# A two-layer sandwich of masked and sign-binarised projections: mask blocks spread on VectorE, and another order of the first unit

## What is computed

```python
# x: (2, 8192, 4096) f32; w1, w2: 4096 x 4096 f32; mask: 4096 x 4096 int32, constant over 32 x 32 blocks
block_mask = mask.reshape(128, 32, 128, 32).sum(axis=(1, 3)) > 0
w1m = w1 * repeat(block_mask, 32 rows, 32 columns)
x = x + layernorm(layernorm(x) @ w1m.T)
x = x + layernorm(layernorm(x) @ sign(w2).T + bias)
```

## Time and profile before

| | us |
|---|---|
| median of 3 runs | 1957.43 (1955.93 to 2028.07) |
| the profiled execution, own time | 1950.22 |
| its span, slowest core | 1948.7 |
| TensorE busy with matmuls | 1859.5 (95%) |
| VectorE busy | 967.1 (50%) |
| ScalarE busy | 484.5 (25%) |
| GpSimd busy | 230.6 (12%) |

### The profile page before, as it was taken

The page is one execution under the profiler, slowest core; times in us unless marked ns, Lnnn a source line. Parts: engine busy times, 40 slices in busy tenths (PEclk is TensorE's granted clock), DMA queues, the critical chain, the costliest instruction groups (busy, mean ns, idle before and its releaser), DMA issues.

```text
span 1948.7 us, 26135 instructions; the slowest of 8 cores (1937.1 to 1948.7 us)
## 1 busy us (share of the span) xinstructions
PE 1859.5 (95%) x9483; PEld 875.6 (45%) x9483; DVE 967.1 (50%) x1441; ACT 484.5 (25%) x449; POOL 230.6 (12%) x420
## 2 busy tenths in 40 slices
PE   2689999999999999999999999999999999999996
PEld 1245444444444444444445444444444444444442
DVE  5778477666564330665533534433552333342465
ACT  2266300000000000133445444434420011110032
POOL 2444100000011000110101000000001011000110
PEclk8899999999999999999999999999999999999998
DMA  9998689976698764787799988898863566562494
GB/s 295 330 311 295 182 284 323 302 220 237 228 313 261 248 200 141 236 257 229 234 274 285 294 275 288 278 314 279 266 213 114 194 227 207 187 200 71 141 284 164
DMA packets 121791, 471.53 MB, mean 242 GB/s; under 512 B 13600, under 2 KB 13616, under 8 KB 106304
## 3 DMA queue, kind: packets, MB, share of 16 engines
q1 hardware_dynamic: 85248, 289.44, 47.4%
q0 software_dynamic: 36416, 180.41, 26.9%
HBM read 354.46 MB, written 115.34 MB: 241 GB/s over the span
## 4 chain that ended last, share of the span: by engine, by line
PE 83%; DMA 9%; DVE 3%; SPq 2%; issue 1%; POOL 1%; ACT 1%; DVEq 0%; ACTq 0%; POOLq 0%
PE pb L474 81%; DMA ST<-w2s 2%; DMA RING<-x 2%; DMA ST<-w1s 2%; PE pb L464 2%; DMA HT<-x 1%; DVE BNX L670 1%; SPq L383 1%; SPq L349 1%; DVE RING L662 1%; DVE RR L638 1%; DMA ST<-mask 0%; DMA ST<-x 0%; PE pb L456 0%; POOL HT L974 0%
## 5 line engine op out<-in xcount | busy, mean ns | idle before, releaser
L474 PE MATMUL pb<-RING,HT 128*128 128x512 bf16 (+1 forms) x8192 | 1786.8, 380 | 21.7 <-DVE RING L662 18.0
L474 PEld LDWEIGHTS pb<-RING,HT 128*128 128x128 bf16 x8192 | 800.3, 98 | 985.9 <-issue 37.8
L760 DVE TENSOR_TENSOR YS<-pb,RR 128x512 bf16<-128x512 f32 x112 | 77.3, 691 | 335.0 <-PE pb L474 334.9
L686 DVE BATCH_NORM_STATS2 BNST<-YS 128x6 f32<-128x512 bf16 x240 | 150.2, 682 | 152.7 <-ACT YS L847 151.5
L847 ACT ACTIVATE YS<-pb 128x512 bf16<-128x512 f32 x128 | 74.7, 600 | 539.7 <-PE pb L474 539.4
L662 DVE TENSOR_TENSOR RING<-ST,ME 128x1024 bf16<-128x1024 f32 x122 | 145.0, 1222 | 102.8 <-PE pb L474 70.4
L853 ACT ACTIVATE RING<-ST 128x1024 fp8e4<-128x1024 f32 x128 | 132.1, 1067 | 179.4 <-DMA ST<-w2s 179.2
L876 ACT ACTIVATE ST<-HT,NM,RS 128x2048 f32<-128x2048 bf16 x32 | 65.7, 2088 | 382.1 <-DVE NM L630 378.7
L638 DVE TENSOR_REDUCE RR<-ST 128x32 f32<-128x1024 int32 x120 | 142.4, 1212 | 25.1 <-DMA ST<-mask 24.3
L837 ACT ACTIVATE HT<-pb 128x1024 bf16<-128x1024 bf16 x128 | 122.3, 1041 | 130.6 <-PE pb L464 130.5
L743 DVE TENSOR_TENSOR HT<-HT,ST 128x1024 bf16<-128x1024 bf16 x64 | 75.6, 1223 | 90.6 <-DMA ST<-x 87.5
(11 more groups left out here) (53 smaller groups left out, 335.1 us busy)
## 6 DMA issues: line engine op xcount, KB each, us to landing
ST<-w2s SPq DMA_DIRECT2D x128, 512.0 KB, 12.5
ST<-w1s SPq DMA_DIRECT2D x122, 512.0 KB, 10.5
ST<-mask SPq DMA_DIRECT2D x120, 512.0 KB, 9.7
ST<-x POOLq DMA_DIRECT2D x64, 512.0 KB, 11.1
out<-ST POOLq DMA_DIRECT2D x32, 1024.0 KB, 6.9
HT<-x SPq DMA_DIRECT2D x24, 1024.0 KB, 20.6
y1d<-YS POOLq DMA_DIRECT2D x32, 512.0 KB, 4.4
c1d<-RING POOLq DMA_DIRECT2D x32, 512.0 KB, 9.0
```

The lines of the kernel that those rows point to most:

```text
L474: ins = t.matmul(bank(b), HT[:, c:c + 128], w[:, e * 512:(e + 1) * 512], start=(first and e == 0), stop=(last and e == 3))
L686: v.bn_stats(BNST[:, c:c + 6], YS[:, i * 512:(i + 1) * 512]).then_inc(sem["bns"], 1)
L760: v.tensor_tensor(YS[:, i * 512:(i + 1) * 512], bank(i), BIA[:, (slab % 2) * 512:(slab % 2) * 512 + 512], op=OP.add).then_inc(sem["ev2"], 1)
```

## The change

1. **Mask layout.** The host puts each 32x32 block of the mask on one partition (1024 numbers in a row), so one reduction gives one sum for a whole block: `mask_piece` writes a 128x1 column of MR. After every two pieces (after 16 for slabs 2 to 7) VectorE compares and repeats the sums over 32 columns (BW) and transposes BW in squares of 32x32 into ME. The matmuls with P4 and SEL, BT, BTD, RR and the semaphores between the engines are gone.
2. **START** no longer moves in units 2 to 7. It is 4 in units 2 to 16, where it was 4, 6, 0, 2, 4, 6 and then 0. In units 16 to 31 it is the old value plus four.
3. **Order of the start.** SyncE loads x tiles 0 to 7 first, then for each of the 8 blocks of slab 0 two mask and two weight pieces, then tiles 8 to 15, with four mask and four weight pieces (blocks 8 and 9) between them, and then the rest of slab 1 in the order mask, mask, weight, weight. TensorE transposes tiles 0 to 7, runs slab 0 over them block by block, and then runs tiles 8 to 15 one after another.
4. **Smaller things.** `x_stats` waits for each half of x by itself; `norm1` does not wait for `norm0`; the normalised halves of tiles 8 to 15 stay where the loaded half lay (`xnormed`); the transposes of tiles 0 to 7 alternate between banks 6 and 7; GpSimd spills unit 0 in one go after `norm1(8)`; `load_x(k, 1)` for tiles 14 and 15 waits until tile k-2 is transposed.

```diff
-
-MASK_END = {2: 2, 3: 3, 4: 4, 5: 5, 6: 6, 7: 7}
-
 START = {2: 4}
 for _u in range(2, 31):
-    if _u in MASK_END:
-        START[_u + 1] = (START[_u] + 2) % 8
-    elif 16 <= _u < 24:
+    if 16 <= _u < 24:
         START[_u + 1] = (START[_u] + 4) % 8
     else:
...
-STAGES = 13
+
+STAGES = 11
+EARLY = 6
...
+    for b in range(8):
+        for e, kind in enumerate("mmww"):
+            put((kind, 2 * b + e % 2), (4 * b + e) % 11)
...
-XHOME = [(k, 8 + k) for k in range(8)] + [(k, "TRW"[(k - 8) % 3]) for k in range(8, 16)]
-
-SEMS = (["cst", "msk_rd", "wgt", "sgn", "rdy_bt", "rdy_me", "msk_mm", "xaggr", "xstat", "xn0", "xn1",
+XHOME = ([(k, 8 + k) for k in range(8)] + [(k, 4 + k) for k in range(8, 12)]
+         + [(k, "TW"[k % 2]) for k in range(12, 16)])
...
-                if h == 0 and k >= 8:
-                    s.wait_ge(sem["xn1"], k - 7)
...
+                if k >= 8:
+
+                    o = k - 8 if k < 12 and h == 0 else k - 4 if k < 12 or h == 0 else k - 2
+                    if k >= 14 or h == 0 or k < 12:
+                        s.wait_ge(sem["tr"], 4 * o + 4)
+                    else:
+                        s.wait_ge(sem["msk_rd"], 16)
+                        s.wait_ge(sem["wgt"], 16)
...
-            load_x(0, 0)
-            load_x(0, 1)
-            for j in range(4):
-                for g in range(4 * j, 4 * j + 4):
-                    load_mask(g)
-                load_x(j + 1, 0)
...
+                            ).then_inc(sem[("ldX%d", "ldH%d")[h] % k], 16)
+
+            for k in range(8):
                 load_x(k, 0)
                 load_x(k, 1)
-            load_x(8, 0)
+            for b in range(8):
+                load_mask(2 * b)
+                load_mask(2 * b + 1)
+                load_w1(2 * b)
+                load_w1(2 * b + 1)
...
+                load_x(k, 0)
                 load_x(k, 1)
...
+                if k in (10, 12):
+                    load_mask(6 + k)
+                    load_mask(7 + k)
+                if k in (11, 13):
+                    load_w1(5 + k)
+                    load_w1(6 + k)
+            for kind, n in FEED[1][EARLY:]:
+                if kind == "m":
+                    load_mask(n)
...
-
-            def start_transposes(k, groups):
-                for g in groups:
-                    if g == 0:
-                        t.wait_ge(sem["xn0"], k + 1)
-                    if g == 2:
-                        t.wait_ge(sem["xn1"], k + 1)
-                    q = 4 * k + g
-                    if q >= 3:
-                        t.wait_ge(sem["tev"], q - 2)
-                    transposes(k, g, 4 + q % 3)
-
-            for j in range(4):
-                t.wait_ge(sem["msk_rd"], 4 * j + 4)
-                if j > 0:
-                    t.wait_ge(sem["rdy_me"], j)
-                mask_sums(7, 0, [j])
-                t.wait_ge(sem["rdy_bt"], j + 1)
-                t.matmul(pb[:, 7 * 512 + 128:7 * 512 + 256], SEL[:, :],
-                         BTD[:, j * 128:(j + 1) * 128], start=True, stop=True
-                         ).then_inc(sem["msk_mm"], 1)
...
+            def start_transposes(k, g):
+                if g == 0:
+                    t.wait_ge(sem["xn0"], k + 1)
+                if g == 2:
+                    t.wait_ge(sem["xn1"], k + 1)
+                q = 4 * k + g
+                if k < 8:
+                    if q >= 2:
+                        t.wait_ge(sem["tev"], q - 1)
+                elif k == 8:
+                    t.wait_ge(sem["ev1"], 4 + g + 1)
+                else:
+                    t.wait_ge(sem["tev"], q - 3)
+                transposes(xnormed(k, g // 2)[:, (g % 2) * 1024:(g % 2) * 1024 + 1024],
+                           6 + q % 2 if k < 8 else 4 + g)
+
+
+            for k in range(8):
+                for g in range(4):
+                    start_transposes(k, g)
+            for b in range(8):
+                for i in range(8):
+                    if b == 0:
+                        t.wait_ge(sem["tev"], 32 if i >= 6 else 4 * i + 4)
+                    if i == 0:
+                        wait_block_ready(t, b)
+                    ins = visit(i, i, b, b == 0, b == 7)
+                    if b == 7:
+                        ins.then_inc(sem["mm"], 1)
+
+            for g in range(4):
+                start_transposes(8, g)
+            for k in range(8, 16):
+                t.wait_ge(sem["ev1"], k - 7 if k < 12 else k - 3)
                 for b in range(8):
-                    if b == 1 and k < 15:
-                        start_transposes(k + 1, range(3))
-                    if b == 4 and k < 15:
-                        start_transposes(k + 1, (3,))
-                    if b == 3 and k == 15:
-                        t.wait_ge(sem["rdy_bt"], 5)
-                        t.matmul(bank(7), SEL[:, :], BTD[:, :], start=True, stop=True
-                                 ).then_inc(sem["msk_mm"], 1)
+                    if k < 15 and b in (3, 6):
+                        for g in ((0, 1) if b == 3 else (2, 3)):
+                            start_transposes(k + 1, g)
+                    if b % 2 == 0:
+                        t.wait_ge(sem["tev"], 4 * k + b // 2 + 1)
                     ins = visit(k % 4, k, b, b == 0, b == 7)
                     if b == 7:
                         ins.then_inc(sem["mm"], 1)
                     elif k == 15:
                         ins.then_inc(sem["blk"], 1)
-                if k == 14:
-                    t.wait_ge(sem["msk_rd"], 32)
-                    t.wait_ge(sem["rdy_me"], 4)
-                    mask_sums(7, 1, range(4))
...
-                        if b == 7 and p == 3 and u in MASK_END:
-                            s = MASK_END[u]
-                            t.wait_ge(sem["msk_rd"], 16 * s + 16)
-                            wait_acc_out(t, u, START[u])
-                            mask_sums(START[u], s, range(4))
-                if u in MASK_END:
-                    masks += 1
-                    t.wait_ge(sem["rdy_bt"], masks)
-                    wait_acc_out(t, u, (START[u] + 1) % 8)
-                    t.matmul(bank((START[u] + 1) % 8), SEL[:, :], BTD[:, :], start=True, stop=True
-                             ).then_inc(sem["msk_mm"], 1)
...
             def mask_piece(g):
-                s, q = g // 16, g % 16
+
+
+                at = g % 32
                 wait_stage_full(v, ("m", g))
-                if q == 0 and s >= 2:
-
-                    v.wait_ge(sem["msk_mm"], 7 if s == 2 else 9 + 2 * (s - 3))
-                v.tensor_reduce(RR[:, (s % 2) * 512 + q * 32:(s % 2) * 512 + q * 32 + 32],
-                                stage(("m", g), True).rearrange("p (a b) -> p a b", b=32),
-                                AX.X, OP.add).then_inc(sem["msk_rd"], 1)
-
-            def mask_bits(b, j0, nj):
-
-                edge(v.tensor_scalar(BT[:, j0 * 16:(j0 + nj) * 16],
-                                     pb[0:32, b * 512 + j0 * 16:b * 512 + (j0 + nj) * 16],
+                v.tensor_reduce(MR[:, at:at + 1], stage(("m", g), True), AX.X, OP.add
+                                ).then_inc(sem["msk_rd"], 1)
+                w = 2 if g < 32 else 16
+                if g % w < w - 1:
+                    return
...
+                v.wait_ge(sem["msk_rd"], g + 1)
+                edge(v.tensor_scalar(BW[:, 0:w * 32].rearrange("p (t i) -> p t i", i=32),
+                                     MR[:, at + 1 - w:at + 1].unsqueeze(2).broadcast_to([128, w, 32]),
                                      0.0, None, OP.is_gt))
-                dst = BTD[:, j0 * 128:(j0 + nj) * 128].rearrange("p (j k n) -> p j k n", j=nj, k=8)
-                bt = BT[:, j0 * 16:(j0 + nj) * 16].rearrange("p (j n) -> p j n", j=nj
-                                                             ).unsqueeze(2).broadcast_to([32, nj, 8, 16])
-                dk = DK[:, :].unsqueeze(1).unsqueeze(3).broadcast_to([32, nj, 8, 16])
-                v.tensor_tensor(dst, bt, dk, op=OP.mult).then_inc(sem["rdy_bt"], 1)
+                c = (g // 16 % 5) * 512 + (g % 16 + 1 - w) * 32
+                edge(v.transpose(ME[:, c:c + w * 32], BW[:, 0:w * 32]))
...
+            for k in range(8):
                 x_stats(k)
-                if k >= 8:
...
+            for b in range(8):
+                mask_piece(2 * b)
+                mask_piece(2 * b + 1)
+                weight_piece(2 * b)
+                weight_piece(2 * b + 1)
+            for k in range(8, 16):
+                x_stats(k)
+                y_stats(0, k - 8)
+                if k in (10, 12):
+                    feed1(FEED[1][3 * (k - 10) // 2:3 * (k - 10) // 2 + 2])
+                if k in (11, 13):
+                    feed1(FEED[1][3 * (k - 11) // 2 + 2:3 * (k - 11) // 2 + 3])
...
-            v.wait_ge(sem["xn1"], 16)
-            for kind, n in FEED[1]:
...
-            masks = 5
+            for b in range(2, 8):
+                feed1(FEED[1][3 * b:3 * b + 3])
+                if b < 6:
```

(31 more changed lines are left out.)

197 lines of the change are left out of this document (50 added, 147 removed).

## The result

The changed kernel takes 1937.74 us (median of 4 runs, 1937.42 to 1939.78). The ratio to before is 0.9905, 95% interval [0.9882, 0.9929], which is 18.6 us of 1957 (13.9 to 23.1). The forecast was 1933: 24.4 us off the median of 1957.4, of which 19.7 came. The profiled execution has a span of 1935.4 us on its slowest core (core 4), and its own time is 1937.42.

The account below looks back on a forecast made before the run. TensorE, busy 95% of the span, was taken to bound the kernel. Mask matmuls -10.2, an earlier unit 2 -15.9 and START +1.7 sum to -24.4 us, from the median of 1957.4 to 1933, range 1922 to 1944.

Parts of the forecast that it names:

- the wait itself: Unit 16, tile 7 now in fourth place instead of eighth: TensorE waits for its transposes' last eviction, +1.7 us.

Follow-up runs that it names:

- e10: Changed kernel with START 0 in units 4 to 16, e9's edits, 28 more identity matmuls a tile and four PSUM banks for early transposes; 1925.2 us, ratio 0.9855.
- e9: Changed kernel with e5's edits and GpSimd's spill(0) moved behind x_scale(9) and norm1(9); 1931.6 us, ratio 0.9883.
- e5: Changed kernel with unit 0's y_stats two tiles later and norm0(9) ahead of the last two evictions of tile 8's transposes; 1938.1 us, ratio 0.9892.

## What to carry to other kernels

A rotation or order table that is changed "by the way" has to be followed to every consumer of the order: here the place of one accumulator decided when a spill went out, and a chain behind it had no slack. A distance read on one core is only good if that core was on time there; read it on all of them. And a gain at the head is worth what the loads behind it let through: e10 started 6.4 us sooner than e9 and was done with unit 12, 740 us later, at the same time. So in this kernel the first change to make, after START, was the program order of GpSimd (one line on top of e5's edits, 3 to 5 us at unit 12 in the profiles), not the pace of the start.

## What the runs showed of the chip

- Around a wait of 2.63 or 2.64 us in unit 16 the clock fell on 7 of 8 cores (244 matmuls in 54.3 to 55.7 us; 52.82 on core 0). The wait's length doesn't settle it: after the longer wait for tile 9 in unit 1 (3.34 to 3.37 us) the next twelve matmuls took 2.75 us, the higher clock, on cores 4, 6 and 7, and the matmuls of the other five were slow (12 in 4.3 to 4.4 us on four of them). The window behind the wait on core 4 and on core 0 of after, the same columns as above:

```profile
1018.40:1022.00 3.60, 3.60 (x10) 1.38 (x11) 0.00 (x0) 3.60 (x5) 0.50 (x1) 0.56 0.56 163
```

```profile
1018.40:1022.00 3.60, 3.60 (x19) 1.60 (x17) 0.00 (x0) 1.89 (x2) 0.28 (x1) 1.00 0.84 182
```

  So the wait cost core 4 4.4 us, and core 0 2.6. The prediction had counted only the wait itself.
- Unit 0 ran at the full clock almost from its first matmul, though on core 4 the transposes right before it had run at the half one (16 in 1.93 us): the granted clock there is 0.50 from 78.00 to 79.68, 0.69 from 79.68 to 80.50 and 1.00 behind that. In before a group of 32 had lost 1.85 us there.
- VectorE transposed 128x64 bf16 in 32x32 squares in 0.25 us. The Trainium skill, VectorE: DVE Perf Modes, section The three transpose paths, has 311 ns for 128x128; the row is for half of that, so the two don't contradict each other.
